# Output projection and last layer norm of a two-layer token mixer: all residuals first, one set of reciprocal roots, weight splits shared between GpSimd and VectorE

## The reference

```python
h = h + _L1_attn_ref(_layernorm(h), ...)        # ends in: y @ Wo.T + bo
h = h + _L1_ffn_ref(_layernorm(h, axis=-1), ...)

def _layernorm(x, axis=-1, eps=1e-05):
    m = jnp.mean(x, axis=axis, keepdims=True)
    v = jnp.var(x, axis=axis, keepdims=True)
    return (x - m) / jnp.sqrt(v + eps)

# _L1_ffn_ref: sigmoid router over 8 experts, top 2, then every expert and one shared MLP
logits = xf @ gate_w.T + lb_bias
scores = jax.nn.sigmoid(logits.astype(jnp.float32))
...
out = out + jnp.where(sel[:, None], y * wmean, 0)      # y = silu(x @ gw.T) * (x @ uw.T) @ dw.T
```

## Time and profile before

| | us |
|---|---|
| median of three runs | 864.26 |
| lowest, highest | 863.16, 865.48 |
| profiled execution, its own time | 865.68 |
| its span in the trace | 863.8 |
| PE / DVE / ACT / POOL busy | 744.2 / 602.8 / 338.9 / 145.2 |

### The profile page before, as it was taken

How to read it: one execution, slowest core, us unless ns; L and a number is a source line. 1 busy time by engine, 2 the same in 40 slices (tenths; PEclk the granted TensorE clock), 3 DMA queues, 4 the chain that set the end, 5 groups by cost and what they waited for, 6 DMA issues and landing times.

```text
span 863.8 us, 14418 instructions
## 1 busy us (share of the span) xinstructions
PE 744.2 (86%) x4818; PEld 631.2 (73%) x4818; DVE 602.8 (70%) x1361; ACT 338.9 (39%) x595; POOL 145.2 (17%) x132
## 2 busy tenths in 40 slices
PE   4548996899999997347999999999847899999997
PEld 4538994699999996235666655553635899999997
DVE  6396667677777777827767767772787777777776
ACT  1305543433333333101766656668134233333332
POOL 0105552000000000436113320211253000000000
PEclk9999996999999999556999999999977999999999
DMA  7300000000000000054353444421400000000000
GB/s 242 124 41 1 1 0 0 1 2 1 1 1 1 0 0 0 1 93 94 72 104 87 98 80 104 90 44 22 185 0 1 1 19 1 19 19 2 20 19 19
DMA packets 21559, 34.77 MB, mean 40 GB/s; under 512 B 6572, under 2 KB 17500, under 8 KB 20960
## 3 DMA queue, kind: packets, MB, share of 16 engines
q1 hardware_dynamic: 16632, 31.60, 13.9%
q10 hardware_dynamic: 4872, 2.46, 1.5%
HBM read 24.03 MB, written 9.99 MB: 39 GB/s over the span
## 4 chain that ended last, share of the span: by engine, by line
PE 75%; DVE 14%; issue 3%; ACT 3%; DMA 3%; SPq 1%; POOL 1%; ACTq 0%; DVEq 0%; POOLq 0%
PE PS L1232 16%; PE PS L1234 16%; PE PS L1233 15%; PE PS L1534 6%; PE PS L1473 6%; PE PS L1491 4%; DVE MX L1133 2%; PE PS L1261 2%; DVE xnp L854 1%; PE PS L1354 1%; PE PS L1563 1%; PE PS L1320 1%; DVE stats L845 1%; DMA KS<-scrH 1%; PE PS L1240 1%
## 5 line engine op out<-in xcount | busy, mean ns | idle before, releaser
L1133 DVE TENSOR_REDUCE MX<-PS 128x1 f32<-128x288 f32 x288 | 125.1, 452 | 50.7 <-PE PS L1473 47.2
L1065 DVE SCALAR_TENSOR_TENSOR h<-PS,cmb,h 128x256 f32<-128x256 f32 (+1 forms) x342 | 143.8, 476 | 0.3 <-PE PS L1234 0.3
L662 ACT ACTIVATE PR<-PS 96x768 f32<-96x768 f32 x144 | 115.3, 806 | 47.2 <-PE PS L1491 45.1
L630 ACT ACTIVATE sg<-PS 128x384 f32<-128x384 f32 x114 | 56.0, 491 | 165.7 <-PE PS L1234 165.7
L1473 PE MATMUL PS<-KS,QS 96*128 96x288 f32 x288 | 97.7, 358 | 17.3 <-DMA KS<-scrH 15.2
L1050 DVE TENSOR_TENSOR al<-aa,ah 128x384 fp32r<-128x384 f32 x114 | 63.6, 558 | 67.2 <-ACT ah L634 67.2
L1473 PEld LDWEIGHTS PS<-KS,QS 96*128 96x128 f32 x288 | 57.2, 202 | 59.1 <-DVE MX L1133 39.3
L634 ACT ACTIVATE ah<-aa 128x384 fp32r<-128x384 f32 x114 | 60.0, 527 | 84.1 <-DVE aa L1044 84.1
L1044 DVE TENSOR_TENSOR aa<-sg,PS 128x384 f32<-128x384 f32 x114 | 63.3, 555 | 26.4 <-ACT sg L630 25.8
L1234 PE MATMUL PS<-xTl,W1h 128*128 128x384 f32 x240 | 81.0, 337 | 0.0
L1232 PE MATMUL PS<-xTh,W1h 128*128 128x384 f32 x240 | 80.8, 337 | 0.0
(11 more groups left out here) (232 smaller groups left out, 1557.9 us busy)
## 6 DMA issues: line engine op xcount, KB each, us to landing
QS<-scrH SPq DMA_DIRECT2D x32, 144.0 KB, 3.9
W1raw<-in_w SPq DMA_DIRECT2D x1, 3840.0 KB, 11.7
W0raw<-in_w SPq DMA_DIRECT2D x1, 3456.0 KB, 10.7
scrH<-qh SPq DMA_DIRECT2D x8, 432.0 KB, 2.5
scrL<-ql SPq DMA_DIRECT2D x8, 432.0 KB, 3.3
QS<-scrL SPq DMA_DIRECT2D x16, 144.0 KB, 4.5
out_tokens<-h SPq DMA_DIRECT2D x6, 384.0 KB, 2.3
x_in<-in_x SPq DMA_DIRECT2D x2, 1024.0 KB, 6.3
```

What stands on the lines that cost most here:

```text
L662: A_(PR[0:KT, c0:c0 + 2, :], PS[0:KT, b:b + 2, 0:CW], ACT.Exp).then_inc(s["e_exp"], 1)
L1065: ins = V.scalar_tensor_tensor(out=hj, in0=PS[:, b + t // 2, (t % 2) * D:(t % 2) * D + D], scalar=cmb[:, ds(g * GT + t, 1), e:e + 1].squee ...
L1133: V.tensor_reduce(MX[:, c // NSH, c % NSH:c % NSH + 1], PS[:, max_bank(it, c), 0:POS], AX_X, ALU.max).then_inc(s["e_mx"], 1)
```

## The change

VectorE now does all six residuals, one set of moments for all 18 tiles, two of the six weight splits (`low_weights`, parts 4 and 5), one reciprocal, and then the rows of all groups. GpSimd does only parts 0 to 3 (`NPW = 4`) and no roots; it no longer waits for moments. ScalarE copies all six parts of `W1h` at once when the weights are there, and takes the square root of the variance (`std`), which VectorE inverts (`invert`); a square root of a constant (`unit`) stands ahead, so that the activation table is changed there. TensorE does all six out projections, twelve warm-up matmuls (`WARM_P = 12`), and then the transposes of groups 0 and 1.

```diff
 # GpSimd
         pool.wait_ge(s["e_yl"], NGQ + 2)
         n1 = sum(WCOLS[1]) // NG
-        root(0)
-        for g in range(NG):
-            if g == 2:
-                root(1)
+        for g in range(NPW):
             z = slice(g * n1, g * n1 + n1)
             pool.wait_ge(s["w_hi1"], g + 1)
             nc.gpsimd.tensor_tensor(W_l[1][:, z], W_raw[1][:, z], W_h[1][:, z].bitcast(F32), ALU.subtract).then_inc(s["w_split1"], 1)
 # ScalarE
         n1 = sum(WCOLS[1]) // NG
+        A_(unit[:, :], unit[:, :], ACT.Sqrt)
         act.wait_ge(s["d_w1"], 16)
-        for g in range(NG + 2):
-            for c in ((0, 1, 2), (3,), (4,), (5,), (), (), (), ())[g]:
-                z = slice(c * n1, c * n1 + n1)
-                A_(W_h[1][:, z], W_raw[1][:, z], ACT.Copy).then_inc(s["w_hi1"], 1)
+        for c in range(NG):
+            z = slice(c * n1, c * n1 + n1)
+            A_(W_h[1][:, z], W_raw[1][:, z], ACT.Copy).then_inc(s["w_hi1"], 1)
+        std(0, NT)
+        for g in range(NG + 1):
             if g < NG:
                 high("p", g, 2 * (g % 3))
             if g:
-                if g <= NG:
-                    logits(1, g - 1, (g - 1) % 2, 6)
+                logits(1, g - 1, (g - 1) % 2, 6)
 # VectorE
+        def low_weights(c):
+            z = slice(c * n1, c * n1 + n1)
+            dve.wait_ge(s["w_hi1"], c + 1)
+            V.tensor_tensor(W_l[1][:, z], W_raw[1][:, z], W_h[1][:, z].bitcast(F32), ALU.subtract).then_inc(s["w_split1"], 1)
         def ready_rows(g):
-            dve.wait_ge(s["rstd_ready"], g // (NG // 2) + 1)
             wait(dve, s["p_T"], g - 1)
             xn_("p", g, xnp[:, g % 2])
-        for g in range(NG // 2):
+        for g in range(NG):
             residual(g)
-        half_moments(0)
-        residual(3)
-        ready_rows(0)
-        residual(4)
-        ready_rows(1)
-        low("p", 0, 0)
...
+        own.settle()
+        moments(0, NT)
+        n1 = sum(WCOLS[1]) // NG
+        for c in range(NPW, NG):
+            low_weights(c)
+        invert(0, NT)
+        ready_rows(0)
+        ready_rows(1)
+        for g in range(NG):
+            low("p", g, 2 * (g % 3))
+            if g + 2 < NG:
+                ready_rows(g + 2)
 # TensorE
-        for g in range(NG - 1):
+        for g in range(NG):
             out_project(g)
+        warm_up(WARM_P)
         late_transposes(0)
-        out_project(NG - 1)
         late_transposes(1)
```

More of the change, by code:

```diff
@@ L28 @@
 REST = NT - GT
-HALF = NT // 2
+NPW = 4
 NE = 8
@@ L116, in build @@
     rstd = keep("rstd", [P, NT])
-    nmr = keep("nmr", [P, NT])
-    minus_half = keep("minus_half", [P, 1])
+    unit = keep("unit", [P, 1])
     bqk0 = keep("bqk0", [P, 4])
@@ L273, in build @@
     names = """d_x0 d_x1 t_det t_T t_ev t_acc d_txt d_const d_wd d_bias d_qkv d_small d_w0 d_w1 d_a1 d_wo d_out
-        dve_own act_own pool_own var_ready std_ready rstd_ready
+        dve_own act_own pool_own var_ready std_ready
         dots_ready dots_sum wex_in wex_ready wts_ready dsc_ready img_done
@@ L403, in _ @@
         nc.gpsimd.memset(ones[:, :], 1.0).then_inc(s["const_pool"], 1)
-        nc.gpsimd.memset(minus_half[:, :], -0.5).then_inc(s["const_pool"], 1)
+        nc.gpsimd.memset(unit[:, :], 1.0).then_inc(s["const_pool"], 1)
         nc.gpsimd.memset(cmb[:, :, :], 1.0).then_inc(s["const_pool"], 1)
[L406 to L410, removed]
         pool.wait_ge(s["const_pool"], 3)
@@ L1191, in residual @@
                 own(bn(g * GT + t, h[:, g * GT + t, :]))
-        def half_moments(n):
-            own.settle()
-            moments(n * HALF, HALF)
+        def low_weights(c):
+            z = slice(c * n1, c * n1 + n1)
+            dve.wait_ge(s["w_hi1"], c + 1)
+            V.tensor_tensor(W_l[1][:, z], W_raw[1][:, z], W_h[1][:, z].bitcast(F32), ALU.subtract).then_inc(s["w_split1"], 1)
         def ready_rows(g):
-            dve.wait_ge(s["rstd_ready"], g // (NG // 2) + 1)
             wait(dve, s["p_T"], g - 1)
             xn_("p", g, xnp[:, g % 2])
-        for g in range(NG // 2):
+        for g in range(NG):
             residual(g)
-        half_moments(0)
-        residual(3)
+        own.settle()
[4 more added lines that the diff above has]
+        invert(0, NT)
         ready_rows(0)
-        residual(4)
         ready_rows(1)
-        low("p", 0, 0)
[L1212 to L1219, removed]
+        for g in range(NG):
+            low("p", g, 2 * (g % 3))
+            if g + 2 < NG:
+                ready_rows(g + 2)
         bias_logits()
@@ L1568, in late_transposes @@
             if g < 3:
-                pe.wait_ge(s["g_res"], g + 4)
+                pe.wait_ge(s["g_res"], NG)
             else:
@@ L1598 @@
 SUM_U, SM_U, REC_U, RO_U, RB_U = [1, 2], 4, 7, 8, list(range(10, 18))
+WARM_P = 12
 S_LEAD = 8
```

## The result

| | before | after |
|---|---|---|
| median (runs) | 863.85 (4) | 850.94 (4) |
| lowest to highest | 863.16 to 865.48 | 848.90 to 852.37 |
| profiled execution / its span | 865.68 / 863.8 | 851.43 / 849.6 |

The ratio is 0.9833, 95% interval 0.9809 to 0.9858: faster, by 12.3 to 16.5 us of 864.26, best estimate 14.4. The forecast was 12.2, just outside that, and 0.9833 × 864.26 = 849.8 lies 0.2 under the range of 850.0 to 855.6. The interval, carried to 864.26, is 847.8 to 852.0, so the measurement can hardly tell the miss from a hit; the median of the four runs, 850.94, even lies inside the range (the quotient of the two medians is 0.9851). The mechanism in the stage was right. What came on top came from places that the forecast had declared untouched.

A forecast was written before the change was run, and what follows sets the result against it. It took TensorE's 16.2 us wait for VectorE's rows, held up by GpSimd's splits, as the bound; carrying the new timeline to the first expert matmul gave 663.28 − 651.05 = 12.2 us, so 864.26 − 12.2 = 852.1, range 850.0 to 855.6.

The forecast's parts named there:

- The wait and its cause: Ahead of the transposes TensorE waits 16.2 us for VectorE's rows, which stand still 14.6 us beside GpSimd's weight splits.
- rival 4: The rows' standstill has another cause than GpSimd; rows stay at 20.8 us, total near before; chance 0.03.
- Out projections and residuals: After attention: six groups take 15.5 us, group 5's residual starts at 628.6, residuals beside splits cost nothing.
- rival 2: GpSimd's splits hold up the residuals too; gain 4.6 us or less, 857 to 862; chance 0.06.
- Moments, splits, reciprocal: VectorE behind the last residual: moments end at 631.7, two splits take 2.8 us, reciprocal 0.3.
- Rival 1: GpSimd's last split runs into the moments, only 0.45 us of room; 852.3 to 854.7, say 853.5; chance 0.22.
- Warm-up: Behind the out projections: 24 records take 7.8 us to 636.2, cost 0.3 and hold TensorE's clock.
- rival 3: TensorE's clock halves from the last out projection on; experts start 6 us later than before, 870.5; chance 0.03.
- Tail: Transposes and routers: router 0 at 638.9, router 5 at 649.0, first expert matmul 2.05 us later.
- The sum: First expert matmul moves from 663.28 to 651.05, so 12.2 us gained.
- Ahead of 612.9 nothing on the path is altered: Before the out projections the change costs or gains nothing; the root's table change falls into ScalarE's 11.47 us wait.
- The sign that stayed silent: The forecast is wrong if the experts' stretch behind the stage, 200 us, changes its length.

The follow-up runs named there:

- e6: Changed kernel with all six weight splits on GpSimd and none on VectorE; 852.81 us, 0.9840 of the kernel before.
- e7: Changed kernel with GpSimd's four splits started only after the moments, beside VectorE's splits and rows; 860.93 us, 0.9925 of the kernel before.
- e5: Changed kernel without the twelve warm-up matmuls; 851.73 us, 0.9833 of the kernel before.
- e1: Changed kernel unaltered, timed again; 848.78 us, 0.9795 of the kernel before.
- e3: Changed kernel with the unused tile `nmr` put back; 853.76 us, 0.9848 of the kernel before.
- e2: Kernel before with only the unused tile `nmr` removed; 861.18 us, 0.9939 of the kernel before.
- e13: Kernel before with an unused tile of 160 bytes added behind `nmr`; 863.17 us, 0.9961 of the kernel before.
- e4: Changed kernel with VectorE's two splits moved behind the last low part, eight warm-ups instead of twelve; 846.09 us, 0.9762 of the kernel before.
- e12: Changed kernel with an unused tile of 256 bytes added ahead of `unit`; 849.10 us, 0.9810 of the kernel before.
- e15: Changed kernel with layer 1's expert weights 32 bytes higher and the tiles behind them 256 bytes higher; 849.60 us, 0.9822 of the kernel before.
- e8: Kernel before with an unused tile of 32 bytes added behind `nmr`; 865.75 us, 0.9990 of the kernel before.
- e11: Kernel before unaltered, timed and profiled again; 865.50 us, 0.9991 of the kernel before.
- e14: Changed kernel with only the experts' and router's intermediate tiles 32 bytes higher; 854.30 us, 0.9877 of the kernel before.

## Why the prediction was right or wrong

- *The wait and its cause.* Right: rows beside splits stand still. The changed kernel, e6 and e7 show it from three sides, and rival 4 is out.
- *Out projections and residuals.* 72 records in 15.78 (15.5 forecast), the residual of group 5 at 626.82, 15.8 behind the first out projection (15.7). Not delayed by the splits: rival 2 is out. (Its range was also wrongly worked out: a gain of 4.6 or less is 859.7 or more, not 857.)
- *Moments, splits, reciprocal.* Two splits 2.89 (2.8; 2 × 1.48 less 0.07 is 2.89 already), moments 1.0. Rival 1 did not happen: splits ended at 628.04, moments began at 628.93, 0.9 of room instead of 0.45.
- *Warm-up.* Ended at 634.5, 7.90 for 24 records (7.8). That they "hold the clock" is right, but worth 0.6 us and not the several that rival 3 made of a fallen clock (e5).
- *Tail.* Router 0 to router 5 took 9.95 (10.1 forecast), experts 2.06 behind (2.05).
- *The sum.* Stage 12.3 against 12.2.
- *The step that failed:* "Ahead of 612.9 nothing on the path is altered", and with it that the 200 us of experts stay as they are. The diff takes out the tile `nmr`; I read that as nothing. It moved the experts' products by 96 bytes and with it TensorE's pace in some 370 us of saturated work. In the first two profiles this shows as layer 0's experts being 1.4 shorter (174.0 to 172.6 from the first to the last matmul by `W0l`) and as the cancelled 1.5 in layer 1. As a whole the addresses are worth 5.0 us by e1 and e3, 5.3 by the ratio of e2 and 2.0 to 3.4 by e13, of which the pace of the experts explains 2.8; where the rest comes from is open. The other 0.5 of the 1.9 us by which the stage began earlier is the sum of 1.4 less ahead of layer 0's experts (161.0 to 159.6) and 0.9 more between the layers (277.9 to 278.8), which nothing here ties to the change.
- *The range.* It reached 2.1 below the forecast, from errors in the stage alone, and held no term for the addresses, 2 to 6 us by these runs. That the time missed it by only 0.2 us is luck: the dip took 1.6 back.
- *The sign that stayed silent.* The forecast was to be wrong "if the experts' stretch itself, 200 us, changes its length": it kept 200.5, because 1.5 gained by the addresses and 1.6 lost to the dip cancelled.
- *The clock behind the stage.* Also not foreseen; it cost 1.6.

## What to carry to other kernels

Before moving work between VectorE and GpSimd, sort VectorE's instructions by what they read: here those with PSUM or a single operand through `bn_stats` lay beside GpSimd's for nothing, while tensor_scalar from SBUF and operations with two SBUF tensors waited for the end of each GpSimd instruction, so GpSimd's bulk belongs beside the first kind. Work that VectorE takes over belongs in its gaps: the same two splits cost 2.4 us of stage ahead of the reciprocal and nothing behind the last evacuation (e4). A diff that adds or drops a tile moves all tiles behind it; compare the length of a saturated stretch, and the records in a fixed window of it, in both profiles before the rest of the difference is given to the change.

## What the runs showed that I had not expected

TensorE's pace at full clock, busy without a gap, depends here on where the experts' intermediate tiles lie: 1002 to 1004 records in 150 us with `sg`, `aa`, `ah` and `al` at multiples of 256 bytes (ten profiles: after, e1, e2, e4 to e7, e12, e13, e15), 990 to 997 with them 32, 64, 96 or 128 bytes beyond one (before, e3, e8 to e11, e14). Over all seventeen the stage begins at 608.4 to 611.2 with the first and at 611.0 to 614.5 with the second; of the 2.6 us between the means layer 0's experts make 1.5. Single records hardly show it (336 against 335 ns); the count in a fixed window does. GpSimd's wait for VectorE in e7 shows as longer busy time (2.90 to 3.47 us a split), not as idle time.
